# Fourteen tables by one-hot matmuls at full batch width and 48 gathers, then four tiles of products and layers

## The reference

```
e = stack([tbl_f[ids[:, f]] for f in range(26)], axis=1)   # 512 x 26 x 128
T = concatenate([r_dense[:, None, :], e], axis=1)          # 512 x 27 x 128
Z = einsum('bnd,bmd->bnm', T, T)                           # products of all pairs
z = Z[:, iu0, iu1]                                         # the 351 pairs above the diagonal
h = concatenate([z, r_dense], axis=1)                      # 512 x 479
h = maximum(h @ W_top1 + b_top1, 0)                        # 512 x 512
h = maximum(h @ W_top2 + b_top2, 0)                        # 512 x 256
y = h @ W_top3                                             # 512 x 1
```

## Time and profile before

| what | value |
|---|---|
| median of 3 runs | 119.73 us (119.35 to 120.79) |
| span of the profiled execution, first to last instruction | 177.3 us |
| the profiled execution's own time beside its span | not given apart from the span |
| mean granted TensorE clock in the profiled execution | 0.788 |
| TensorE busy with matmuls | 97.7 us |
| VectorE busy | 54.0 us |
| ScalarE busy | 53.0 us |
| GpSimd busy | 73.9 us |
| DMA moved | 11.96 MB |

### The profile page before, as it was taken

The page is one execution under the profiler, slowest core; times in us unless marked ns, Lnnn a source line. Parts: engine busy times, 40 slices in busy tenths (PEclk is TensorE's granted clock), DMA queues, the critical chain, the costliest instruction groups (busy, mean ns, idle before and its releaser), DMA issues.

```text
span 177.3 us, 3454 instructions
## 1 busy us (share of the span) xinstructions
PE 97.7 (55%) x1494; PEld 82.6 (47%) x1494; DVE 54.0 (30%) x128; ACT 53.0 (30%) x105; POOL 73.9 (42%) x79
## 2 busy tenths in 40 slices
PE   2239988192284001000000046999995999489695
PEld 0127656171272000000000036989884999389583
DVE  3369567144024100000005001474756202302131
ACT  7252544250250001000031000644642634174041
POOL 4877777787777777777777000000000000000000
PEclk9999999879558555555555555799999699879999
DMA  4999753315225121212125100000000000000000
GB/s 138 268 259 351 182 154 81 129 46 162 59 53 169 45 59 44 59 44 59 50 54 159 31 0 4 4 0 2 4 0 7 0 4 0 4 4 0 7 4 0
DMA packets 6661, 11.96 MB, mean 67 GB/s; under 512 B 3091, under 2 KB 4115, under 8 KB 6518
## 3 DMA queue, kind: packets, MB, share of 16 engines
q1 hardware_dynamic: 4342, 7.02, 14.2%
q0 software_dynamic: 2304, 4.72, 9.9%
HBM read 11.73 MB, written 0.00 MB: 66 GB/s over the span
## 4 chain that ended last, share of the span: by engine, by line
PE 41%; issue 26%; another core or an unknown queue 19%; ACT 7%; DMA 5%; POOL 1%; DVE 1%
PE ps_prod L626 8%; PE ps_turned L604 8%; PE ps_turned L605 7%; PE ps_turned L589 5%; DMA sb_rows<-in_tbl,sb_ids 3%; PE ps_mlp L657 3%; PE ps_pack L657 3%; ACT sb_feats L296 2%; ACT sb_table_hi L513 2%; PE ps_mlp L559 2%; PE ps_pack L559 2%; DMA sb_ids<-in_ids 1%; POOL sb_rows L439 1%; ACT sb_feats L288 1%
## 5 line engine op out<-in xcount | busy, mean ns | idle before, releaser
L439 POOL DMA_INDIRECT sb_rows<-in_tbl,sb_ids x72 | 73.1, 1015 | 23.4 <-issue 21.6
L626 PE MATMUL ps_prod<-sb_feats 128*28 128x26 f32 x1024 | 15.2, 201 | 54.1 <-issue 39.3
L604 PE MATMUL ps_turned<-sb_one_hot,sb_table_hi 125*128 125x512 f32 (+2 forms) x80 | 34.0, 429 | 12.2 <-issue 7.4
L626 PEld LDWEIGHTS ps_prod<-sb_feats 128*28 128x28 f32 x1024 | 12.5, 114 | 56.9 <-issue 41.3
L605 PE MATMUL ps_turned<-sb_one_hot,sb_table_lo 125*128 125x512 f32 (+2 forms) x80 | 32.1, 406 | 0.0
L479 DVE TENSOR_SCALAR sb_one_hot<-sb_id_less_8p 125x512 fp32r<-125x512 f32 (+2 forms) x80 | 25.8, 381 | 12.3 <-remote 7.6
L468 DVE TENSOR_TENSOR sb_table_lo<-sb_table,sb_table_hi 125x1024 fp32r<-125x1024 f32 x10 | 12.3, 1226 | 53.8 <-issue 37.6
L604 PEld LDWEIGHTS ps_turned<-sb_one_hot,sb_table_hi 125*128 125x128 f32 x80 | 18.8, 235 | 15.3 <-issue 8.1
L296 ACT COPY sb_feats<-ps_turned 128x512 f32<-128x512 f32 (+2 forms) x10 | 9.1, 908 | 49.1 <-remote 35.0
L288 ACT COPY sb_feats<-ps_turned 128x512 f32<-128x512 f32 (+2 forms) x15 | 15.2, 1026 | 25.9 <-remote 20.1
L605 PEld LDWEIGHTS ps_turned<-sb_one_hot,sb_table_lo 125*128 125x128 f32 x80 | 18.9, 236 | 1.6
(11 more groups left out here) (74 smaller groups left out, 80.6 us busy)
## 6 DMA issues: line engine op xcount, KB each, us to landing
sb_table<-in_tbl SPq DMA_DIRECT2D x10, 448.0 KB
sb_rows<-in_tbl,sb_ids POOLq DMA_INDIRECT x72
sb_w<-in_W_top SPq DMA_DIRECT2D x1, 1024.0 KB
sb_table<-in_tbl SPq DMA_DIRECT2D x10, 52.0 KB
sb_w<-in_W_top SPq DMA_DIRECT2D x1, 512.0 KB
sb_dense<-in_r_dense SPq DMA_DIRECT2D x1, 256.0 KB, 4.5
sb_ids<-in_ids SPq DMA_DIRECT2D x1, 52.0 KB, 2.1
sb_w<-in_W_top SPq DMA_DIRECT2D x1, 1.0 KB
```

The source lines that it names most:

```text
L439: pool.indirect_dma_start(rows[:, row_at[t, s], :], None, tables[f], bass.IndirectOffsetOnAxis(ids_sb[:, t, f:f + 1], 0)).then_inc(rows_in ...
L604: pe.matmul(turned_ps[:, i % 2, 0:w], table_hi[:, j % SPLITS, c, :], hot, start=(c == 0), stop=False)
L626: done = pe.matmul(prod_ps[quad * QUAD:quad * QUAD + SLOTS, i, 0:NF - 1], feats[:, t, at:at + SLOTS], feats[:, t, at:at + NF - 1], start=T ...
```

## The change

- Fourteen tables, all those of 1000 rows, are chosen instead of ten, and each for all 512 samples at once. The products of no tile begin before all 27 features of all samples are in `feats`.
- The other twelve tables are gathered: 48 gathers instead of 72, issued table by table (four tiles each). TensorE turns one table's four tiles into one bank.
- The ids are no longer turned and spread by matmuls. A DMA for each chosen table reads its row of 512 ids and writes it to all 128 partitions (256 KB written); three buffers. The ids with the samples on the partitions are still loaded for the gathers, now laid out on the host.
- Three PSUM banks instead of two for choosing and turning; four table buffers instead of three. ScalarE alone copies all 27 banks into `feats`.
- After that, the four tiles go through products, packing and layers in a fixed order, with two buffers each for products, spread, packed, pairs and both hidden layers. There are no special steps for the last tile. The three parts of a packing are now split by run: ScalarE has four copies, VectorE three.
- w3, b1 and b2 are laid out on the host.

The core of the new code (the loops on TensorE, VectorE and ScalarE after the setup):

```diff
+ITEMS = """
+D h0 h1 r0 h2 r1 h3 h4 r2 h5 r3 h6 r4 h7 r5 h8 r6 h9 r7 h10 h11 r8 h12 r9 h13 r10 r11
+""".split()
...
+            def load_wide(j):  # sync
+                f = chosen[j]
+                if j >= WIDE:
+                    sp.wait_ge(near_ready, j - WIDE + 1)
+                sp.dma_start(ids_wide[:, j % WIDE, :],
+                             ids_of_table[f:f + 1, :].broadcast_to([P, B])).then_inc(wide_in[j % WIDE], 16)
...
+            for g, f in enumerate(gathered):  # gpsimd
+                for t in range(TILES):
+                    pool.indirect_dma_start(
+                        rows[:, g, t, :], None, tables[f],
+                        bass.IndirectOffsetOnAxis(ids_sb[:, t, f:f + 1], 0)).then_inc(rows_in[g], 16)
...
+            for j in range(NCH):  # vector
+                half = CHUNKS[j] // 2
+                dve.wait_ge(near_ready, j + 1)
+                for c in range(half):
+                    hot(j, c)
+                if j == 0:
+                    low(0)
+                for c in range(half, CHUNKS[j]):
+                    hot(j, c)
+                if j + 1 < NCH:
+                    low(j + 1)
...
+            spread_pack(0)
+            spread_pack(1)
+            pairs_out(0)
+            spread_pack(2)
+            pairs_out(1)
+            spread_pack(3)
+            pairs_out(2)
+            pairs_out(3)
...
+            make_near(0)  # scalar
+            high(0)
+            make_near(1)
+            high(1)
+            for i, item in enumerate(ITEMS):
+                empty(i)
+                if item[0] == "h" and int(item[1:]) + 2 < NCH:
+                    make_near(int(item[1:]) + 2)
+                    high(int(item[1:]) + 2)
...
+            def turn(i, item):  # tensor
+                bank_free(i)
+                if item == "D":
+                    pe.wait_ge(dense_in, 16)
+                else:
+                    pe.wait_ge(rows_in[int(item[1:])], 16 * TILES)
...
+            for i, item in enumerate(ITEMS):
+                if item[0] == "h":
+                    choose(i, int(item[1:]))
+                else:
+                    turn(i, item)
+            pe.wait_ge(blanks_ready, 4)
+            pe.wait_ge(emptied, len(ITEMS))
+            pe.wait_ge(weights_in, 80)
+            products(0)
+            products(1)
+            turn_pack(0)
+            layer1(0, 0)
+            layer1(0, 1)
+            products(2)
+            turn_pack(1)
+            layer1(1, 0)
+            layer1(1, 1)
+            layer2(0)
+            products(3)
+            layer3(0)
+            turn_pack(2)
+            layer1(2, 0)
+            layer1(2, 1)
+            turn_pack(3)
+            layer2(1)
+            layer1(3, 0)
+            layer3(1)
+            layer1(3, 1)
+            layer2(2)
+            layer2(3)
+            layer3(2)
+            layer3(3)
```

More of the change, by code:

```diff
@@ L53 @@
 ]
-PACK_PARTS = [range(0, 1), range(1, 4), range(4, 7)]
+ACT_PACKS = (0, 4, 5, 6)
+DVE_PACKS = (1, 2, 3)
 def pack_order():
@@ L67, in pack_order @@
     return order
[L72 to L86, removed]
[5 rows of a table removed]
[L92 to L102, removed]
-def slot_plan(table_rows):
[L108 to L116, removed]
+def slot_plan(table_rows):
+    chosen = [f for f, r in enumerate(table_rows) if r % PARTS == 0 and r <= MOST_ROWS]
+    chosen.sort(key=lambda f: table_rows[f])
+    gathered = [f for f in range(len(table_rows)) if f not in chosen]
+    return [0] + [f + 1 for f in gathered + chosen], chosen, gathered
 def w1_rows(table_rows, depth):
@@ new lines, in load_table @@
+            def load_table(j):
+                n = CHUNKS[j]
+                src = tables[chosen[j]].rearrange("(p c) d -> p c d", c=n)
+                if j >= TABLES_AHEAD:
+                    sp.wait_ge(lo_ready, j - TABLES_AHEAD + 1)
+                cut = PARTS // 16 * 16
+                for a, b in ((0, cut), (cut, PARTS)):
+                    sp.dma_start(table[a:b, j % TABLES_AHEAD, 0:n, :], src[a:b]).then_inc(table_in[j % TABLES_AHEAD], 16)
+            sp.dma_start(ids_sb[:, :, :], ids).then_inc(ids_in, 16)
@@ new lines, in products @@
+            def products(t):
+                if t >= 2:
+                    pe.wait_ge(spread_ready, 2 * (t - 1))
+                for i in range(QUAD):
+                    for quad in range(P // QUAD):
+                        at = (quad * QUAD + i) * SLOTS
+                        done = pe.matmul(prod_ps[quad * QUAD:quad * QUAD + SLOTS, t % 2, i, 0:NF - 1],
+                                         feats[:, t, at:at + SLOTS], feats[:, t, at:at + NF - 1],
+                                         start=True, stop=True)
+                done.then_inc(prods_ready, 1)
@@ new lines, in layer2 @@
+            def layer2(t):
+                pe.wait_ge(h1_ready, M1 * (t + 1))
+                if t == TILES - 1:
+                    pe.wait_ge(pairs_ready, TILES)
+                elif t >= 1:
+                    pe.wait_ge(y_ready, t)
+                for c in range(M2):
+                    for k in range(M1):
+                        done = pe.matmul(h2_ps(t)[:, c * P:(c + 1) * P], w2[:, k, c * P:(c + 1) * P], h1[:, t % 2, k, :],
+                                         start=(k == 0), stop=(k == M1 - 1))
+                    done.then_inc(h2_summed, 1)
@@ new lines, in layer3 @@
+            def layer3(t):
+                pe.wait_ge(h2_ready, M2 * (t + 1))
+                for k in range(M2):
+                    done = pe.matmul(y_ps(t), w3[:, k:k + 1], h2[:, t % 2, k, :], start=(k == 0), stop=(k == M2 - 1))
+                done.then_inc(y_summed, 1)
+            pe.wait_ge(ident_ready, 1)
+            for i, item in enumerate(ITEMS):
+                if item[0] == "h":
+                    choose(i, int(item[1:]))
+                else:
+                    turn(i, item)
```

625 lines of the change are left out of this document (227 added, 398 removed), and 5 rows, old and new, of the table STEP_NAMES.

## The result

| | before | after |
|---|---|---|
| median of 5 runs | 119.73 us (119.35 to 121.41) | 141.35 us (139.62 to 144.85) |
| ratio after to before | | 1.1735, 95% interval 1.1643 to 1.1827 |
| profiled execution: time, span | span 177.3 us | 144.85 us, 142.7 us |

The change makes the kernel 21.6 us slower. The forecast was 128.0 us with a range of 119 to 135: the sign was right, the size was not. The profiled execution is the longest of the five; the spans of the other four were 137.4 to 139.4 us.

The account below looks back on a forecast made before the run. Before was held bound by gathers and TensorE's chain at 98 to 99 us, then a 16 us tail. For the new kernel, front 73.4 + back 50.6 + 4.2 around made 128.2, forecast 128 us, range 119 to 135.

Parts of the forecast that it names:

- front: Stage completing all features before the first product: TensorE sets the pace, 4.35 us per table, ending at 73.4 us.
- back: Products, packing and layers of four tiles after the last gather: 42.7 work + 5.4 waits + 2.5 end = 50.6 us.
- around: Launch and end outside the span, plus what the clean chain of before leaves out: 4.2 us, bounds 0 and 5.8.
- on the edge: Last gathered rows land at 67.6 to 72 us, hidden under the front; last group is turned at 72.0 either way.
- my own signs: Signs in the new profile: no wait for `sb_table` or wide ids; wrong if the front waits for loads.
- Bound on two sides at once: Kernel before: TensorE's chain and GpSimd's gathers both end by 98 to 99 us, then a tail of 16.
- the idle middle: TensorE almost idle from about 58 to 102 us in before's profile; claimed recording effect, absent from timed runs.
- One pause per tile: Products in the back: one code fetch pause of 2.1 us per tile, 4.5 us products per tile, bounds 2.4 and 6.6.
- the second rival: Front starved of table and id loads, TensorE's clock falls, plus 5 to 15 us: 133 to 143; chance 0.10.
- the tail: End of before, from turning tile 3's last group at 99.3 us to the span's end: 16.2 us.
- the first rival: Pauses inside products come only from recording; back 4 x 2.1 us shorter, time 119.8 to 121.4; chance 0.13.
- The third: Rival: recording lengthens all compute engines' work, so timed engines run faster; 115 us with 12%; chance 0.07.

Follow-up runs that it names:

- the limited kernel: The kernel after, with GpSimd's gathers held to two tables under way: 140.93 us (139.33 to 143.59), ratio 1.1776.
- the two kernels with half of them: Kernel after with half the gathers, weights last and bfloat16 `feats`: 151.5 us; the limited kernel with products of 64 of 128 samples per tile: 124.63 us.
- its limited version: The kernel before, with GpSimd's gathers held to two groups (8 gathers) under way: 120.65 us (118.65 to 121.54).

## Why the prediction was wrong

The sum was 73.4 (front, copies included) + 50.6 (back) + 4.2 (around) = 128.2. With the same cut, at the first product, the recorded execution of after is 83.3 + 59.4 + 2.15 = 144.85. That of the limited one, whose median is the same within its runs, is 77.1 + 59.8 + 2.4 = 139.3. So in the clean case the front was 3.7 more, the back 9.2 more, the surroundings 1.8 less.

**What held.** The gathers got shorter and ceased to count. The last ended at 68.3 in after where I had 66.1, and 24 of them left out changed nothing. In the limited kernel the last rows came at 74.7, where TensorE waited 0.4 us for them: "on the edge", as I had it. TensorE set the pace of the front: 4.1 us from table to table in the limited kernel, where I had 4.35. In the limited kernel ScalarE waited for ids only at the start (4.1 us); in the recorded execution of after it waited a second time (2.8 us), beside the late table, which by my own signs counts against me. The back of four tiles came into the open and outweighed the gain, which is the whole of the sign. Layer 2 took 1.79 us per tile, as computed. From the end of the products to layer 1, tiles 0 to 2 took 2.1 us each, where I had 0.5 for transposes and 1.8 of waiting. "Bound on two sides at once" is made likely and not shown: one gather less bought nothing, and two less, with a changed order, cost 7 us and moved the chain to TensorE; the run with half of the gathers that was to decide it had the idle middle.

**The step that failed: the back.** Two of its terms.

- *One pause per tile.* I priced 4 x 2.1 = 8.4 us, from the single pause in tiles 1 and 3 of before. There were five, 2.21 + 2.02 + 1.74 + 1.92 + 2.21 = 10.1 us: three in tiles 0 and 1, whose products follow one another with 1024 instructions, and one each in tiles 2 and 3. I had named two pauses per tile as the upper bound and hadn't used it for just these tiles. Plus 1.7.
- *The high clock throughout.* All durations of the sum came from stretches of before in which TensorE was full. In after the pauses and the waits for ScalarE and VectorE follow one another, and the granted clock of the first window is 0.57. The products took 11.6 us instead of 9.4 (plus 2.2), layer 1 5.19 + 6.13 + 5.46 + 1.79 + 1.98 = 20.55 instead of 14.4 (plus 6.2). This is the largest term, and I had weighed a low clock only for a starved front (the second rival). Nothing in the sum asked what the gaps that I myself had put into the back would do to the clock.

With 0.8 less for waits and transposes together and nothing to speak of for the rest, this gives the 9.2. That the pauses go with the number of instructions is shown by the two kernels with half of them. That the granted clock was low is read from the rows. What pulled it down is not separated: half of the products means fewer pauses and also fewer short matmuls, the waits for VectorE stand among them, and a pause alone didn't always do it (in the recorded execution of after tile 2's layer 1 ran at the high clock behind a pause of 2.25 us, in the limited kernel behind one of 2.21 it didn't).

**The front** began late: 13.2 in place of 8.0, since I had overlooked that the dense rows stand first in the order and land late, plus 5.2. From there the last chosen table was done after 60.7 us, where I had 64.0, so the faster pace gave back 3.3. Behind it I had 1.4 for one group turned and copied; in the limited kernel two groups were still to be turned, with a short wait for rows and the copies, 3.2 us, plus 1.8. In the profiled execution, with its late table, the front ended 6.2 us later still. Whether the late table comes from the crowd on the DMA engines wasn't separated: with the weights last the first product stood at 77.4, no earlier.

**The surroundings.** Undisturbed executions of before have spans of 117.0 to 119.5 for times of 118.8 to 121.3, so 1.8 us lie around the span, not 4.2. The missing 2.4 belong into before's chain: in its limited version the last rows are landed and turned at 101.3 and the tail is 17.0, against my 99.3 and 16.2. I carried them to the new kernel's sum as surroundings, where they were 1.8 too much; by luck this hid a part of what front and back lacked.

**Readings.** The slices with a low clock that I named in the second rival are wrong: in the earlier trace rows they are 11, 12 and 14 to 25. The 18 ns of the first rival are two weight loads with two matmuls; one of each took 9.2 ns.

**The idle middle** of before I held for the recording's work. That was wrong: it is there unrecorded as well. The sum left it out all the same, which was right for the runs that it was to forecast, though not for the reason that I gave; and the profile of after, where I had said that it should show, has none.

**The rivals.** The first, a code fetch that costs nothing because the pause is the recording's, is refuted: the pauses are in each trace, their number follows the instructions, and recorded executions are as long as unrecorded ones (139.33 recorded beside 140.19 to 143.59). That they are fetches of code the trace doesn't say outright: in the back of the limited kernel nine packets of 16 KB come from the queue of instructions, one of them 0.2 to 0.6 us ahead of each of the five pauses, and the other four where there is no pause. The spacing of 256 instructions fits what I cited of the Trainium skill ("Runtime: NRT & Kernel Launch", instruction fetch mechanics), blocks of 16 KB. Its remark that the crossing is mostly hidden doesn't hold here where products follow one another: 256 instructions pass in 1.2 to 1.7 us and the pause behind them, 1.7 to 2.4 us, is as long or longer. The second rival gave the right size for a wrong place: the clock did fall, but in the back. The third, engines faster unrecorded, is out: of the four executions of the limited kernel after the recorded one, 139.33, is the shortest.

## What to carry to other kernels

When a stage is moved out of the shade of another, price it at the clock that its own gaps will leave, not at that of a full stretch: read the granted clock of a window that has the same gaps. Count pauses by instructions in a fast stretch, not by tile. Before a gap called "issue" is counted as one, look whether another engine's work that the program waits for ends right at its end. And look at the order of the queues first: here the transposes in the middle of the next tile's products, with each copy of pairs ahead of the next spread, gave back 10 of 21 us. By the traces these are some 4 us of waits, 4 us of layer 1 (17.6 in place of 22.0) and 3.5 us of pauses (five still, 7.6 in place of 11.1), while the products themselves took 1.4 longer.

## What the runs showed that I had not expected

- The kernel before, with 72 gathers issued without a wait, took 180 us in place of 120 in three of five groups of experiments, with TensorE idle for 38 us on end while GpSimd went on at 1.25 us per gather. With a wait behind each group of gathers the idle middle was gone (161.6 beside 182.8, with 49 us of waits added). A limit of two groups under way cost nothing, 120.65 beside 119.81, but was run only where there was no middle to remove.
- A quiet gather of 128 rows lands 2.5 us after its start, in the loaded front 7 to 8 us.
- ScalarE's copy of 128x512 out of PSUM took 2.63 us on the mean with bfloat16 results, 1.19 with float32.
- The DMA engines carried 210 to 340 GB/s from slice 2 to 19 of after and weren't what its chain waited for, the dense rows at the start and one late table excepted.
